# Two cost entries and the tie width of a list scheduler, in an eight-core attention and feed-forward kernel

## What is computed

```python
def attn(x):                                   # x: (4, 8192, 1024)
    q  = x @ Wq + bq
    kv = (x @ Wdown + bdown) @ Wup + bup       # latent of 256
    # 16 heads of 64; k, v = halves of kv
    att = softmax(einsum('bthd,btgd->bthg', q, k) / 8)   # heads against heads
    out = einsum('bthg,btgd->bthd', att, v)
    return out.reshape(B, T, D) @ Wout + bout

def ffn(x):                                    # hidden 3072
    h = silu(x @ wg.T / 127) * (x @ wu.T / 127)
    return h @ wdn.T / 127

x = layernorm(x + attn(x))
x = layernorm(x + ffn(x))
```

## Time and profile before

| | us |
|---|---|
| two runs | 3522.4 and 3683.82, median 3603.11 |
| the profiled execution | 3529.78 |
| its span on core 6, first to last instruction | 3527.8 |
| TensorE busy | 2693.5 (76%), 12416 matmuls |
| VectorE busy | 1670.4 (47%) |
| ScalarE busy | 801.0 (23%) |

### The profile page before, as it was taken

The page is one execution under the profiler, slowest core; times in us unless marked ns, Lnnn a source line. Parts: engine busy times, 40 slices in busy tenths (PEclk is TensorE's granted clock), DMA queues, the critical chain, the costliest instruction groups (busy, mean ns, idle before and its releaser), DMA issues.

```text
span 3527.8 us, 41206 instructions; the slowest of 8 cores (3489.8 to 3527.8 us)
## 1 busy us (share of the span) xinstructions
PE 2693.5 (76%) x12416; PEld 1061.5 (30%) x12416; DVE 1670.4 (47%) x2454; ACT 801.0 (23%) x1361; POOL 292.1 (8%) x540
## 2 busy tenths in 40 slices
PE   0000686789887989799978987898889887989566
PEld 0000212233333333334333333333333333333222
DVE  2221355355546545464637454655555545554312
ACT  0000310142214120513042303330242124221101
POOL 0111000001100110011001100010001000110110
PEclk9999956699999999999999999999999998999678
DMA  7887200212322232312241224223322322232222
GB/s 199 240 238 206 48 1 24 41 47 63 96 72 82 63 81 75 95 55 81 72 114 49 72 81 103 60 60 93 89 71 63 93 69 80 62 93 63 89 80 81
DMA packets 108701, 303.92 MB, mean 86 GB/s; under 512 B 16192, under 2 KB 24768, under 8 KB 108496
## 3 DMA queue, kind: packets, MB, share of 16 engines
q1 hardware_dynamic: 61520, 169.14, 17.3%
q0 software_dynamic: 46976, 132.15, 13.3%
HBM read 269.77 MB, written 39.85 MB: 88 GB/s over the span
## 4 chain that ended last, share of the span: by engine, by line
PE 62%; DMA 12%; issue 6%; DVE 6%; ACT 4%; DVEq 0%; ACTq 0%; POOLq 0%; POOL 0%; SPq 0%
PE P L448 10%; PE P L762 9%; PE P L395 9%; PE P L405 9%; PE P L778 8%; PE P L671 7%; DMA wgb<-wg_s 4%; DMA wub<-wu_s 3%; PE P L344 2%; DMA wqb<-wq_s 2%; PE P L816 2%; DVE p_sb L725 2%; DMA wob<-wout_s 2%; PE P L613 2%; PE P L585 2%
## 5 line engine op out<-in xcount | busy, mean ns | idle before, releaser
L725 DVE TENSOR_TENSOR p_sb<-P,vdup_all 128x512 bf16<-128x512 f32 x1024 | 695.5, 690 | 430.2 <-PE P L778 303.1
L395 PE MATMUL P<-x_bf,wgb 128*128 128x512 bf16 x1536 | 533.9, 411 | 117.0 <-DMA wub<-wu_s 95.7
L405 PE MATMUL P<-x_bf,wub 128*128 128x512 bf16 x1536 | 514.1, 403 | 38.9 <-DVE h_sb L421 38.9
L778 PE MATMUL P<-p_sb,id_sb 128*128 128x256 bf16 x2048 | 481.9, 293 | 23.4 <-DVE p_sb L725 16.6
L448 PE MATMUL P<-h_sb,wdb 128*128 128x512 bf16 x1536 | 480.0, 381 | 15.4 <-DVE r_bf L457 14.1
L762 PE MATMUL P<-e_sb,selz_sb 16*128 16x512 bf16 x1024 | 413.3, 413 | 57.2 <-DVE e_sb L707 29.4
L646 DVE TENSOR_TENSOR hadb<-q_sb,krep 128x2048 bf16<-128x2048 bf16 x256 | 309.9, 1224 | 243.3 <-PE P L671 144.9
L671 PE MATMUL P<-hadb,selred_sb 128*16 128x256 bf16 x2048 | 325.7, 275 | 34.7 <-ACT e_sb L658 20.5
L421 DVE TENSOR_TENSOR h_sb<-s_sil,P 128x512 bf16<-128x512 bf16 x192 | 131.0, 682 | 412.2 <-PE P L405 284.5
L311 PE MATMUL P<-x_bf,wd_sb 128*128 128x512 bf16 x128 | 37.2, 442 | 351.8 <-DMA x_bf<-xt 351.7
L414 ACT ACTIVATE s_sil<-P 128x512 bf16<-128x512 f32 x192 | 114.4, 597 | 760.9 <-PE P L395 742.5
(11 more groups left out here) (69 smaller groups left out, 1926.1 us busy)
## 6 DMA issues: line engine op xcount, KB each, us to landing
wdb<-wdn_s SPq DMA_DIRECT2D x64, 768.0 KB, 4.8
wgb<-wg_s POOLq DMA_DIRECT2D x192, 256.0 KB, 3.0
wub<-wu_s POOLq DMA_DIRECT2D x192, 256.0 KB, 3.0
wob<-wout_s SPq DMA_DIRECT2D x128, 256.0 KB, 3.2
wqb<-wq_s SPq DMA_DIRECT2D x64, 256.0 KB, 3.0
yt<-x2b SPq DMA_DIRECT2D x64, 256.0 KB, 2.2
stg<-wg SPq DMA_DIRECT2D x24, 512.0 KB, 5.3
stg<-wu SPq DMA_DIRECT2D x24, 512.0 KB, 5.2
```

Of the source, the lines that this page charges most:

```text
L395: e.matmul(o, l, r, start=st, stop=sp)),
L405: e.matmul(o, l, r, start=st, stop=sp)),
L725: add('V', (lambda e, o=o, a=a, b=b: e.tensor_mul(o, a, b)), waits=w, inc=s_v, d=640)
L778: e.matmul(o, id_sb[:, :], r, start=st, stop=sp)),
```

## The change

Three numbers. The broadcast matmul (L762) is planned at 380 ns in place of the default of 260. The gather matmul (L778) is planned at 170 ns in place of 152. The class of the scheduler's key is 400 ns wide in place of 200. No instruction is added, removed or changed; only the order of the two chains on each engine can come out differently, and the numbers that the semaphores are waited for with it.

```diff
                             add('T', (lambda e, o=o, l=l, r=r:
                                       e.matmul(o, l, r, start=True, stop=True)),
-                                waits=w, inc=s_pe)
+                                waits=w, inc=s_pe, d=380)
...
                             add('T', (lambda e, o=o, r=r, st=(g == 0), sp=(g == NH - 1):
                                       e.matmul(o, id_sb[:, :], r, start=st, stop=sp)),
-                                waits=w, inc=s_pe, d=152)
+                                waits=w, inc=s_pe, d=170)
...
-                key = (round(es / 200.0), -CP[id(nd)], es)
+                key = (round(es / 400.0), -CP[id(nd)], es)
```

## The result

| | before | changed |
|---|---|---|
| median, us | 3536.52 (10 runs) | 3569.39 (11 runs) |
| lowest, us | 3521.65 | 3560.0 |
| profiled execution, us | 3529.78 | 3574.18 |
| ratio | | 1.0102, 95% interval 1.008 to 1.0124 |

The changed kernel is 1.0% slower, about 36 us. The medians are of all runs, while the ratio leaves out those in which one die showed a lower clock, as did one of the two behind the median of 3603.11 shown ahead of the prediction.

A forecast was written before the change was run, and what follows sets the result against it. TensorE's order was taken as the bound with both chains in play. Early fills 3.2 plus emptied sums 2.4 made 5.6 us a stage, +39 us over seven stages on 3530: 3570 us, own range 3525 to 3623, overall 3480 to 3645.

The forecast's parts named there:

- (a): Early in each stage: the wider class drops 15 of 39 small feed-forward fills, done later in full stretches; +3.2 us a stage.
- (b): Sums of half 0: attention runs ahead longer, the `h_sb` stall grows, 11 feed-forward matmuls move later; +2.4 us a stage.
- The bound, and where the change can act: Seven two-chain stages, 367.9 us each: TensorE's order is the bound there; the change can act only in these.
- (c): Products once in balance: 2.8 feed-forward matmuls a step instead of 2.5; 0 us, transfers adding up to 1 a stage.
- (d): VectorE and ScalarE: wider class lets attention pass a ready feed-forward instruction; 0 us, bounds -0.7 and +0.7.
- Grouping rival: Scores of half 1: wide class groups feed-forward matmuls into runs, saving shape changes; -42 to -80 us, 3485 us; chance 0.20.
- No-effect rival: Extra time and lost fills fall where transfers or the norm hold TensorE anyway; 3530 to 3545 us; chance 0.25.
- Clock rival: Products: attention first runs alone at 1.2 GHz, the mixed stretch starts low; 14.7 us a stage, 3633 us; chance 0.18.

## What was right in the prediction, and what was not

The forecast was 3570 us, +39 on the profiled 3529.78. The median is 3569.39, the ratio puts the change at +36, the stage periods of the profiled cores at +42. Set beside the two-run median of 3603.11, 3570 would be a faster kernel. The prediction worked from 3529.78 and from a slowdown, and the ten-run median of 3536.52 bears that choice out.

The step that failed is the sum of (a) and (b), 3.2 + 2.4 us a stage. It moved 15 + 11 = 26 matmuls into full stretches and let nothing come back. In the streams 38 more stand in the products, which got 5.0 and 4.2 us longer, and another 1.4 came up around the projection of half 0; against that, 4.3 us came back in the scores, the sums and the norm, where the sum had nothing. With too little loss in it and no gain, the sum came to 5.6 where 6.2 was measured; that these two errors cancelled is luck. The cause given in (a) failed too: the wide class by itself took none of the 37 fills away and made the stage 2.8 us shorter. The costs by themselves carry the loss (stage +7.4 us).

By its steps:

- **The bound, and where the change can act: right.** Seven stages, 373.9 us instead of the 373.5 forecast, the products full in both kernels.
- **(a) Fewer small fills: the count right, the cause and one price not.** 37 fills became 22, the 15 that were forecast. But the class alone leaves all 37: with the old costs the scores of half 0 take 22 feed-forward matmuls instead of 16. The costs alone leave 35. It needs both. And I let a dropped fill give back 0.1 us at most; scores and sums of half 0 got 1.8 us shorter.
- **(b) Emptied sums: right in kind, too small in number.** TensorE waits 9.2 us a stage instead of 4.8, with the `h_sb` product behind the chain, though the row shows it at L762 and not at L405. 17 matmuls were lost there, not 11: 3.7 us instead of 2.4 at the same price.
- **(c) The rest of the products: 0 forecast, not quite.** There were 2.4 matmuls a step instead of 2.8, and TensorE waited 2.1 us a stage more for products in half 0. The longer waits for weights (+4 us, at most 1 forecast) showed no price of their own.
- **(d) Classes on the other engines: 0 forecast, -1.2 us measured** in the first norm (10.0 to 8.8 us), beyond my bound of -0.7. The class alone gives -0.5, the costs alone nothing.
- **Grouping rival:** the class didn't group (417 runs in the scores of half 1 instead of 434), as argued. Its price was nearly right: 8.3 us a stage when runs were made, where 48 fewer runs at 0.2 would be 9.6.
- **No-effect rival** (3530 to 3545 us): falls, since the interval begins at 1.008, 3558 us.
- **Clock rival:** right as a mechanism and wrong about where. With the costs alone it takes 5 us a stage in the products of half 0 (9.6 us more at the low clock), in the changed kernel nothing. There J = 0 holds 24 feed-forward matmuls and 2.2 us at the low clock; with the costs alone it holds 8, and 11.7 us. I could not tell these two apart from the trace of the kernel before. Its last sentence, by which activity releases the clock and the trace agrees, is true only of the stages with both chains: the earlier trace rows themselves show 0.50 with TensorE busy 17.46 and 17.98 of 20 us.

Of the +9.2 us in the products of the two halves, 38 moved matmuls at 0.22 would make 8.4; in half 0 that price is an average over a first J that got shorter and seven that got longer. What came back is 1.8 us in the scores and sums of half 0, 1.1 in the scores of half 1 and 1.4 in the last part with the norm.

## What to carry to other kernels

A planned cost that is nearer to the measured one need not give a better order: here 380 ns for a matmul that takes 410, with 170 for one that takes 110, made one chain's path longer, and that shifted when the other chain got its turn, which is all that a list scheduler does with it. When two chains share an engine, ask of each edit how many instructions move from stretches with idle time into full ones, what comes back where they left, and what the granted clock is in the stretch behind one that was left empty. And look at what alternation itself costs; keeping the turn on TensorE was worth 2.5% of this kernel, and the best setting of the edited numbers that was run 0.4%.

## What the runs showed that I had not expected

- TensorE's clock fell to 0.50 and stayed there while the engine was busy 8.94 of 9 us with broadcast and gather matmuls and 2 of the feed-forward, and went on at 0.50 through a J with 8 feed-forward matmuls among them; the J's of half 0 with 18 and more behind it ran at 1.00 but for 0.9 us in the first.
- A J of products at 0.50 with 2 feed-forward matmuls took 9.5 us, with 8 of them 12.0 us; at 1.00 with 17 it took 9.0 to 9.5. So 15 more feed-forward matmuls in a J took no time there, at the other level of the clock.
- Each half's new costs alone cost 1.0 to 1.2%, both together 1.0%.
